# Turning the attention probabilities of batches 2 to 5 by VectorE and DMAs instead of TensorE, in a fused cross-attention and quantised feed-forward kernel

## The reference

```python
# attention, per batch; theta_w, phi_w, g_w: 128 x 256, T = 512
theta_x = theta_w @ ctx + theta_b            # from ctx_2048[b]
phi_x   = phi_w @ layernorm(x[b]) + phi_b
scores  = theta_x.T @ phi_x                  # 512 x 512
p       = softmax(scores, axis=-1)
g_x     = g_w @ layernorm(x[b]) + g_b
t_x     = p @ g_x.T                          # 512 x 128, kept as 128 x 512
h       = relu((t_x - mean) * rsqrt(var + 1e-5) * gamma + beta)   # mean, var over all of t_x
x       = x + tanh(g_xattn) * (out_w @ h + out_b + ctx)
# feed-forward, over all 2048 rows of 512
x       = x + tanh(g_ffn) * ffn(layernorm(x))
# ffn: silu(q(x) @ q(w1)) * (q(x) @ q(w2)), then q(.) @ q(w3); ternary weights, 8-bit activations
```

## Time and profile before

| | us |
|---|---|
| median of 3 runs (298.07 to 298.43) | 298.15 |
| profiled execution, its own time | 298.3 |
| its span, first to last instruction | 296.5 |
| busy in the span: PE / DVE / POOL / ACT | 291.0 / 239.8 / 197.8 / 195.5 |
| granted TensorE clock, mean over the span | 1.00 |

### The profile page before, as it was taken

One profiled execution on the slowest core, in us unless ns is written; L12 is line 12 of the kernel. 1 busy time (PEld: TensorE's weight loads), 2 busy tenths in 40 slices (PEclk: granted clock), 3 DMA queues, 4 the chain that ended last, 5 costly groups with the idle time before them and its releaser, 6 DMA issues.

```text
span 296.5 us, 4393 instructions
## 1 busy us (share of the span) xinstructions
PE 291.0 (98%) x1310; PEld 155.6 (52%) x1310; DVE 239.8 (81%) x539; ACT 195.5 (66%) x319; POOL 197.8 (67%) x302
## 2 busy tenths in 40 slices
PE   8999999999999999999999999999999999999996
PEld 5665757575757565644444444444444444444444
DVE  3797888989898786999889787986986896867872
ACT  2388888989898898799765645465456456345620
POOL 3353598959593958657798777786786786655710
DMA  7999587858594001010335374334343362651355
GB/s 261 414 416 410 200 277 292 282 153 330 167 343 143 0 2 35 1 39 0 71 71 62 87 140 106 63 81 106 72 97 83 76 107 68 131 116 29 83 100 180
DMA packets 56535, 42.23 MB, mean 142 GB/s; under 512 B 43456, under 2 KB 46656, under 8 KB 55488
## 3 DMA queue, kind: packets, MB, share of 16 engines
q1 hardware_dynamic: 56224, 41.69, 48.8%
q10 hardware_dynamic: 288, 0.27, 0.3%
HBM read 24.65 MB, written 6.82 MB: 106 GB/s over the span
## 4 chain that ended last, share of the span: by engine, by line
PE 79%; DVE 6%; POOL 4%; issue 3%; DMA 3%; ACT 2%; SPq 1%; POOLq 0%; DVEq 0%
PE bank L1238 37%; PE bank L1256 14%; PE bank L1182 8%; PE bank L1154 5%; PE bank L1199 4%; PE bank L1118 3%; PE bank L1169 3%; PE bank L1131 2%; DMA x<-x_dram 2%; PE bank L1141 2%; POOL stage L401 2%; PE bank L1269 1%; DMA probT<-prob 1%; POOL prob L385 1%; DVE blocks L772 1%
## 5 line engine op out<-in xcount | busy, mean ns | idle before, releaser
L1238 PE MATMUL bank<-wq,stage 128*128 128x512 bf16 x512 | 113.3, 379 | 0.0
L1238 PEld LDWEIGHTS bank<-wq,stage 128*128 128x128 bf16 x512 | 50.1, 98 | 61.6 <-issue 2.3
L872 DVE SCALAR_TENSOR_TENSOR stage<-bank,s,stage 128x512 f32<-128x512 f32 x64 | 47.6, 744 | 22.6 <-PE bank L1238 18.6
L615 ACT ACTIVATE xn<-stage 128x1024 f32<-128x1024 f32 x31 | 32.8, 1057 | 46.0 <-DVE stage L872 46.0
L607 ACT ACTIVATE stage<-bank,s 128x512 f32<-128x512 f32 x64 | 43.1, 680 | 16.5 <-PE bank L1238 14.4
L1256 PE MATMUL bank<-wq,prob 128*128 128x512 bf16 x224 | 50.5, 379 | 0.0
L467 POOL TENSOR_SCALAR stage<-stage,hsc 128x1024 f32<-128x1024 f32 x30 | 33.3, 1119 | 20.6 <-DVE hsc L903 20.6
L877 DVE TENSOR_REDUCE m<-stage 128x1 f32<-128x1024 f32 x31 | 37.7, 1216 | 0.8
L1256 PEld LDWEIGHTS bank<-wq,prob 128*128 128x128 bf16 x224 | 21.9, 98 | 26.5
L1154 PE MATMUL bank<-ph,th 128*128 128x512 f32 x96 | 34.4, 471 | 0.2 <-DVE ph L753 0.2
L473 POOL TENSOR_SCALAR prob<-stage 128x1024 bf16<-128x1024 f32 x30 | 30.9, 1044 | 0.0
(11 more groups left out here) (122 smaller groups left out, 460.4 us busy)
## 6 DMA issues: line engine op xcount, KB each, us to landing
stage<-w1t_dram SPq DMA_DIRECT2D x4, 1024.0 KB, 11.7
stage<-w2t_dram SPq DMA_DIRECT2D x4, 1024.0 KB, 8.5
stage<-w3t_dram SPq DMA_DIRECT2D x4, 1024.0 KB, 6.7
x<-x_dram SPq DMA_DIRECT2D x7, 512.0 KB, 8.4
c_sb<-ctx_in_dram SPq DMA_DIRECT2D x7, 512.0 KB, 7.2
out_dram<-stage SPq DMA_DIRECT2D x14, 256.0 KB, 2.4
spill<-blocks SPq DMA_DIRECT2D x5, 512.0 KB, 2.6
placed<-spill SPq DMA_DIRECT2D x20, 128.0 KB, 2.8
```

The source lines that it names most:

```text
L615: A.activation(junk, h_sb[t % 2][:, half * HF:(half + 1) * HF], ACT.Square, accum_out=ssq[:, half:half + 1]).then_inc(sq_done, 1)
L872: V.scalar_tensor_tensor(h_sb[k][:, c * 512:(c + 1) * 512], up_banks(n)[1][:, :], s12[:, u % 2, 1, k:k + 1], sil[n % 3], ALU.mult, ALU.mul ...
L1238: last = mm(bank[:, :], turned[:, row:row + P], wq[:, at:at + 512], start=q == 0, stop=q == KI - 1)
```

## The change

`first_block(i)` says from which chunk on a batch is turned by blocks: chunk 2 for batch 1 as before, chunk 1 for batch 2, chunk 0 for batches 3, 4 and 5, none for batches 0, 6 and 7. So seven `turn_p` (28 transposes) and seven `p_copy` go, and seven `turn_blocks` come. All `values` of a chunk that is turned by blocks run after `phi(i + 2)`: for batches 3 to 5 four in a row. The DMAs of `move_blocks` grow with the chunks: 0.75 MB out and 0.75 MB back for batch 2 and 1 MB each way for batches 3 to 5, where it was 0.5 MB. Three things are reordered besides: on DVE, `x_stats(1, 0)` goes behind the theta `low_part` of batch 0; on ACT, the third slot of step 1 goes behind `exp(1, 2)`; on SP, `load_c(7)` goes ahead of `load_weight(2, 2)`. The bounds of the semaphore counts (`turn_no`, `block_no`) follow.

```diff
-        blocks = sb("blocks", [P, TC * 2 * P])
-        placed = sb("placed", [P, 4, 2 * P])
-        spill = nc.dram_tensor("spill", [P, TC * 2 * P], F32, kind="Internal").ap()
-        spill_v = spill.rearrange("(q b) (k r) -> k b q r", b=32, k=4)
+        blocks = sb("blocks", [P, TC * 4 * P])
+        placed = sb("placed", [P, TC * 4 * P])
+        spill = nc.dram_tensor("spill", [P, TC * 4 * P], F32, kind="Internal").ap()
...
+        def first_block(i):
+
+            return 2 if i == 1 else 1 if i == 2 else 0 if 3 <= i <= B - 3 else TC
+
         def by_blocks(i):
 
-            return 1 <= i <= B - 3
+            return first_block(i) < TC
...
         def turned_p(i, c):
 
-            if by_blocks(i) and c >= 2:
-                return placed[:, :, (c - 2) * P:(c - 1) * P].rearrange("s q (c r) -> s q c r", c=TC)
+            if c >= first_block(i):
+                n = TC - first_block(i)
+                return placed[:, 0:TC * n * P].rearrange("s (q k c r) -> s k q c r", q=4, k=n, c=TC)[:, c - first_block(i)]
...
             def move_blocks(i):
 
-                sp.wait_ge(blocks_ready, 2 * i)
+                n = TC - first_block(i)
+                sp.wait_ge(blocks_ready, block_no(i))
                 if i >= 2:
                     sp.wait_ge(blocks_moved, 64 * (i - 1))
-                sp.dma_start(spill[:, :], blocks[:, :]).then_inc(blocks_out, 16)
+                sp.dma_start(spill[:, 0:TC * n * P], blocks[:, 0:TC * n * P]).then_inc(blocks_out, 16)
                 sp.wait_ge(blocks_out, 16 * i)
                 sp.wait_ge(tx_done, i)
                 for k in range(4):
-                    sp.dma_start(placed[32 * k:32 * (k + 1)], spill_v[k]).then_inc(blocks_moved, 16)
+                    back = spill[:, k * n * P:(k + 1) * n * P].rearrange("(q b) r -> b q r", b=32)
+                    sp.dma_start(placed[32 * k:32 * (k + 1), 0:TC * n * P].rearrange("b (q r) -> b q r", q=4), back)\
+                        .then_inc(blocks_moved, 16)
...
             move_blocks(4)
+            load_c(7)
             load_weight(2, 2)
-            load_c(7)
             load_weight(2, 3)
             move_blocks(5)
...
                 if i >= 1:
-                    p_copy(i - 1, 0)
-                    p_copy(i - 1, 1)
+                    for c in range(min(first_block(i - 1), 2)):
+                        p_copy(i - 1, c)
...
                 exp(i, 1)
-                if i == 1:
-                    slot(i, 2)
                 if whole:
                     p_copy(i - 1, 3)
                 exp(i, 2)
+                if i == 1:
+                    slot(i, 2)
...
             def first_steps(i):
                 if i == 1:
                     sum_inverse(0)
-                x_stats(i + 1, 0)
+                if i == 1:
+                    x_stats(2, 0)
                 low_part(i, th, b_th, 0, th_ready, thl_ready)
                 if i == 0:
+                    x_stats(1, 0)
                     low_part(0, ph, b_ph, 1, ph_ready, phl_ready)
...
-                if by_blocks(i - 1):
-                    turn_blocks(i - 1, 0)
-                    turn_blocks(i - 1, 1)
+                for c in range(first_block(i - 1), TC):
+                    turn_blocks(i - 1, c)
                 low_part(i, ph, b_ph, 1, ph_ready, phl_ready)
...
             def values(i, c):
-                if by_blocks(i) and c >= 2:
+                if c >= first_block(i):
                     pe.wait_ge(blocks_moved, 64 * i)
...
-                if by_blocks(i - 2):
-                    values(i - 2, 2)
-                    values(i - 2, 3)
+                if i >= 2:
+                    for c in range(first_block(i - 2), TC):
+                        values(i - 2, c)
...
-                if i >= 1:
+                if i >= 1 and first_block(i - 1) > 0:
                     turn_p(i - 1, 0)
                 scores(i, 0)
-                if i >= 1:
+                if i >= 1 and first_block(i - 1) > 1:
                     turn_p(i - 1, 1)
...
-                elif i >= 1:
+                elif i >= 1 and first_block(i - 1) > 0:
                     values(i - 1, 0)
                 scores(i, 2)
...
-                elif i >= 1:
+                elif i >= 1 and first_block(i - 1) > 1:
                     values(i - 1, 1)
                 scores(i, 3)
```

More of the change, by code:

```diff
@@ L764, in sum_inverse, with turn_blocks @@
                 V.reciprocal(rsum[:, :], esum[:, :]).then_inc(rsum_ready, 1)
-            def turn_blocks(i, k):
-                if k == 0:
+            def turn_blocks(i, c):
+                n = TC - first_block(i)
+                if c == first_block(i):
                     dve.wait_ge(pnorm_ready, 4 * i + 4)
@@ L771, in turn_blocks @@
                         dve.wait_ge(blocks_out, 16 * (i - 1))
-                V.transpose(blocks[:, :].rearrange("p (s k c r) -> p k c s r", s=4, k=2, c=TC)[:, k],
-                            prob[:, i % 2, :, (2 + k) * P:(3 + k) * P].rearrange("p c (s r) -> p c s r", r=32))\
+                V.transpose(blocks[:, 0:TC * n * P].rearrange("p (s k c r) -> p k c s r", s=4, k=n, c=TC)[:, c - first_block(i)],
+                            prob[:, i % 2, :, c * P:(c + 1) * P].rearrange("p c (s r) -> p c s r", r=32))\
                     .then_inc(blocks_ready, 1)
@@ L944, in third_step @@
                 low_part(2, th, b_th, 0, th_ready, thl_ready)
-                turn_blocks(1, 0)
-                turn_blocks(1, 1)
+                for c in range(first_block(1), TC):
+                    turn_blocks(1, c)
                 low_part(2, ph, b_ph, 1, ph_ready, phl_ready)
```

4 lines of the change are left out of this document (3 added, 1 removed).

## The result

The changed kernel took **305.5 us** (median of 4 runs, 305.02 to 306.05), the kernel before 298.23 on the same chip: a ratio of 1.0246, with an interval of 1.0234 to 1.0258. It is 2.5% slower where 0.6% was forecast, and outside the range of 298.0 to 302.0. The profiled execution took 305.24 us with a span of 303.4; its granted clock was 0.999, that of the other three 0.994 (305.02 us, the fastest) and 1.00 twice, so the clock is not the cause.

The account below looks back on a forecast made before the run. The prediction took the x loop, with DVE nearly equal, to bound the steps. Shifts of +0.3, +0.3 and three of +0.35 us sum to +1.65, 298.3 to 300.0; 0.15 less for the median gives 299.9 us, range 298.0 to 302.0.

Parts of the forecast that it names:

- the loop: Steps 4 to 6: tx_dev on DVE to ready x, phi, moved values, next tx_dev; 14.78 us a step.
- DVE: Seven more turn_blocks of some 0.65 us: busy time up by 4.5 us, a step of 14.72 to 14.73 us.
- X(3): Start of tx_dev on DVE in step 3: 0.3 us later than 49.35, at about 49.7.
- X(4): Start of tx_dev on DVE in step 4: 0.6 us later in all, at 64.5.
- The first steps: Reorders in steps 0 and 1: turn of batch 1 shifted between -0.8 and +0.1 us, taken as -0.3.
- The DMAs: Blocks out and back in about 9.1 to 10.8 us where 10.3 are there: in time, 1 us to spare.
- the sum: For the blocks' DMAs: 0.5 MB more costs 1.3 us out and 1.3 back, about 9.1 us in all.
- the bound: For the blocks' DMAs: 2 us more each way at the read back's 264 GB/s, 10.8 us in all.
- case C: Rival: blocks come late, 0.5 to 1.3 us for each of three batches, 301.5 to 304 us; chance 0.11.
- The loads of w3 and c: load_weight(2, 2) goes out some 3 us later, its ACT slot up to 1 us late: nothing net, at most +0.5.
- Case A: Rival: PE decides, 3.3 us leave with the transposes plus the early 0.3 to 0.8, 294.5 to 295 us; chance 0.14.

Follow-up runs that it names:

- e1_first_steps: The kernel before with only x_stats(1, 0) behind the theta low_part and the third weight slot of step 1 behind exp(1, 2): 298.12 us, 0.9990.
- e8_three_chunks: The changed kernel with first_block at 1 for batches 2 to 5, so three chunks by blocks and one turned by PE: 301.39 us, 1.0096.
- e14_three_small_w3: The changed kernel with three chunks by blocks for batches 2 to 5 and w3 loads cut to an eighth: 297.61 us, 0.9977.
- e5_small_w3: The changed kernel with blocks whole and each w3 load cut to 64 of its 512 columns: 302.13 us, 1.0131.

## Why the prediction was wrong

- **PE does not decide; the loop does.** Right, once the blocks are in time. PE lost its transposes and waited, 0.46 us each, for `x_norm` in front of `phi` in two steps of the changed kernel. With the transfers of before the steps are 14.80 and 14.81 us against 14.78, and the whole is 300.27 and, in the other way of taking the DMAs out, 299.82, against 299.9.
- **DVE.** Nearly right: 3.7 us of busy time more, not 4.5. Four turns in a row take 2.42 us (59.54 to 61.96), the 0.61 for each that the prediction took.
- **X(3) and X(4).** X(4) came at 64.63, forecast 64.5. X(3) came later than forecast (50.14, not 49.7). In this execution the phi `low_part` of step 0 began at 10.72, where `e1_first_steps`, with the same order, has it at 10.21. That half microsecond does not come with the change: `e8_three_chunks` and `e14_three_small_w3`, which are the same up to there, have 10.14 and 10.23, and X(3) at 49.57 and 49.64. That X(4) is right is partly luck: X(3) was 0.4 us late, and the step behind it took 14.49 us, 0.3 less than the 14.8 forecast.
- **The first steps, -0.3.** The size is right (the turn of batch 1 is 0.32 earlier in `e1_first_steps`), but the time shows 0.1%, at the edge of what can be told. The slot's move brings none of it.
- **"The DMAs ... I take the first, as larger pieces lift the read's rate: in time, with 1 us to spare."** This is the step that failed, in two terms. The price of the read back was mis-sized. Before, it took 4.1 us; the sum added 1.3 for the second half and the bound 2.0, and it took 7.5, 3.4 more. From the end of the turn of batch 3 (61.96, where the phi `low_part` begins) to its `values` (73.47) it was 11.5 us, where the sum had 9.1 and the bound 10.8; PE was ready after 10.4, and 10.3 was forecast. Larger pieces did not lift the rate: 225 GB/s at a full share, below the 264 of the bound, which at a full share would be some 310 (an estimate from rows 10). The argument that kept case C at 0.11, that the rate of 264 was set by the pace of issue, was read from one window with a share of 0.85, and it was wrong: the share is 1.04 to 1.06 when more bytes are in flight, at the same pace of issue. With w3 out of the way this term alone is worth 2.3 us (`e5_small_w3`, 302.13, against 299.82).
- **"The loads of w3 and c ... Nothing net; to +0.5 at most."** The second term. It priced the swap of two loads and was nearly right about that. It did not price what the larger blocks do to the loads: each goes out later (67.73 for 64.82 the first; 85.00 for 79.49 the third, of which 4.8 us are the later read back of batch 4 in front of it, 82.53 for 77.69), takes 10.3 us instead of 6.7, and is still running when the next blocks want to leave. The writes of batches 4 and 5 took 6.0 and 7.0 us instead of 3.85, and ACT waited 4.6 us for w3. The prediction had the queueing of batch 4's write in case C, and that of batch 5's nowhere. Taking w3 out of the changed kernel gives 3.4 us back (305.50 to 302.13).
- **Case C** was the mechanism, and PE waiting for `placed` was named as its sign. It was priced as a wait for each batch by itself, 0.5 to 1.3 us, to 304 at most. The waits were 1.13, 1.63 and 0.91, but they feed on each other: the late blocks delay SP's queue, this delays w3, w3 delays `exp` and the next blocks, and the interaction is some 1.5 us.
- **Case A** is not quite without ground: three chunks without w3 give steps of 13.97 us. It needs DMA time that this stretch does not have. (Its own sum, 3.3 and 0.3 to 0.8 us off 298.15, gives 294.0 to 294.6, a little lower than it says.)

## What to carry to other kernels

When work moves from a compute engine to DMAs, add up the time of the DMA engines over the whole step, with the loads that were hidden there, and not only the latency of the new transfer against its deadline. A share of 0.85 in a window of small transfers was no reserve here: twice the bytes went slower, not faster. Where the two ends of such an estimate lie on both sides of the deadline, plan for the worse one; here even that was 0.7 us too good. A second queue did not help where the engines behind it were full; the order in which the transfers were let go did. And look at the granted clock of every run before you put a loss down to waiting alone: a long wait of PE cost the wait and then, in some runs, half the clock behind it.
